# Batched matmul plus residual on one core: four batches for each transfer, four 4 MB rooms, loops of a whole ring

## What is computed

```python
x: (64, 128, 2048) fp32;  itok_B_0_15: (64,) int32 in 0..15;  L0_cond_weights: (16, 128, 128) fp32
W = weights[condition]
return x + jnp.einsum('bct,bcd->bdt', x, W)
```

## Time and profile before

| | |
|---|---|
| median of 3 runs | 322.93 us (322.84 to 416.34) |
| the profiled execution | 322.95 us, of which 321.2 us is the span |
| PE busy | 244.9 us (76% of the span), 512 matmuls |
| DVE busy | 146.7 us (46%), 64 sums |
| POOL busy | 19.0 us (6%) |
| DMA | 135.27 MB, 421 GB/s over the span |
| mean granted TensorE clock | 0.934 |

### The profile page before, as it was taken

One profiled execution on the slowest core, in us unless ns is written; L12 is line 12 of the kernel. 1 busy time (PEld: TensorE's weight loads), 2 busy tenths in 40 slices (PEclk: granted clock), 3 DMA queues, 4 the chain that ended last, 5 costly groups with the idle time before them and its releaser, 6 DMA issues.

```text
span 321.2 us, 2655 instructions
## 1 busy us (share of the span) xinstructions
PE 244.9 (76%) x512; PEld 102.1 (32%) x512; DVE 146.7 (46%) x64; POOL 19.0 (6%) x69
## 2 busy tenths in 40 slices
PE   0699999788868787696986867876869868678630
PEld 0244444233323233242332322332324323223310
DVE  0056757742545534346252555343552525553350
POOL 0000101000000000000000000000000000000000
PEclk9999999997989999789897999997997979999795
DMA  7999999999999999999999999999999999999994
GB/s 294 433 439 388 435 426 426 431 437 433 428 424 433 437 433 426 426 433 441 428 426 428 437 435 428 424 431 439 431 428 426 431 439 433 426 428 435 437 426 208
DMA packets 9362, 135.27 MB, mean 421 GB/s; under 512 B 1042, under 2 KB 1042, under 8 KB 1042
## 3 DMA queue, kind: packets, MB, share of 16 engines
q10 hardware_dynamic: 4754, 68.16, 49.8%
q1 hardware_dynamic: 4608, 67.11, 49.0%
HBM read 68.16 MB, written 67.11 MB: 421 GB/s over the span
## 4 chain that ended last, share of the span: by engine, by line
DMA 82%; PE 9%; DVE 3%; issue 1%; SPq 1%; DVEq 0%
DMA x_ring<-x 82%; PE product L97 9%; DVE x_ring L114 3%; SPq L70 1%; DVEq L114 0%; SPq L66 0%; DVEq L113 0%; SPq L65 0%; SPq L64 0%; SPq L69 0%
## 5 line engine op out<-in xcount | busy, mean ns | idle before, releaser
L97 PE MATMUL product<-x_ring,chosen_weights 128*128 x512 | 244.9, 637 | 63.3 <-DVE x_ring L114 43.4
L114 DVE TENSOR_TENSOR x_ring<-product,x_ring 128x2048 f32 x64 | 146.7, 2292 | 164.1 <-PE product L97 164.1
L97 PEld LDWEIGHTS product<-x_ring,chosen_weights 128*128 128x128 f32 x512 | 102.1, 203 | 205.3 <-issue 205.2
L83 POOL COPY chosen_weights<-weight_table 128x128 f32 x64 | 18.8, 293 | 269.0 <-DVEq L113 155.3
L138 POOL MEMSET const-float32-0.0<- 128x1 f32 x1 | 0.1, 98 | 0.1
L138 POOL MEMSET const-bfloat16-1.0<- 128x1 bf16 x1 | 0.1, 102 | 0.0
L138 POOL MEMSET const-uint8-127<- 128x1 uint8 x1 | 0.1, 102 | 0.0
L138 POOL MEMSET const-float32-1.0<- 128x1 f32 x1 | 0.1, 98 | 0.0
L138 POOL BASE_LOAD x1 | 0.0, 12 | 0.1
## 6 DMA issues: line engine op xcount, KB each, us to landing
x_ring<-x SPq DMA_DIRECT2D x32, 2048.0 KB, 19.4
out<-x_ring ACTq DMA_DIRECT2D x32, 2048.0 KB, 19.2
weight_table<-weights ACTq DMA_DIRECT2D x1, 1024.0 KB, 4.9
condition_row<-condition ACTq DMA_DIRECT2D x1, 0.2 KB
```

What stands on the lines that cost most here:

```text
L83: pool.tensor_copy(chosen_weights[b][:, :], weight_table[:, bass.ds(state * features, features)]).then_inc(weights_chosen, 1)
L97: last = pe.matmul(product[:, b % psum_slots, m * BANK_COLUMNS:(m + 1) * BANK_COLUMNS], chosen_weights[b][:, :], x_ring[:, bass.ds(ring_co ...
L114: dve.tensor_tensor(tile, product[:, b % psum_slots, :], tile, AluOpType.add).then_inc(psum_free, 1)
```

## The change

A group is now four batches: the host lays four side by side, a row is 32 KB, a group 4 MB, and there are 16 groups. `x_ring` has the same 16 MB, in four rooms. The loops of PE, DVE and POOL count four turns of 16 batches, so that one turn goes once round the ring and the addresses in `x_ring` don't depend on the turn. There are 16 `chosen_weights` instead of four, and each batch of a turn has its own `weights_chosen`, `product_done` and `sum_done` semaphore. DVE no longer raises a semaphore of its own for POOL; POOL waits for `product_done` itself. SP and ACT have no loop: their transfers are written out one by one. A load waits only for the store that last used its room. A store waits only for the last sum of its group. The last group is stored in four pieces, one for each batch, each as soon as its own sum is done.

```diff
-GROUP = 2
-IN_FLIGHT = 2
-RING_TURNS = 4
+GROUP = 4
+ROOMS = 4
-    per_turn = IN_FLIGHT * GROUP
+    per_turn = ROOMS * GROUP
-        x_ring = sbuf("x_ring", [channels, RING_TURNS * IN_FLIGHT * group_columns])
+        x_ring = sbuf("x_ring", [channels, ROOMS * group_columns])
...
+        def sums_wanted(turn, b):
+            return turn + (2 if b >= per_turn - psum_slots else 1)
         @block.sync
-            for g in range(IN_FLIGHT):
-                sp.sem_inc(x_loaded[g], 16)
-                sp.sem_inc(room_free[g], 16 * RING_TURNS)
-            with sp.Fori(0, turns) as turn:
-                for g in range(IN_FLIGHT):
-                    sp.wait_ge(x_loaded[g], 16 * (turn + 1))
-                    sp.wait_ge(room_free[g], 16 * (turn + 1))
-                    sp.dma_start(ring_group(turn, g), dram_group(x, turn, g)
-                                 ).then_inc(x_loaded[g], 16)
+            for g in range(groups):
+                room = g % ROOMS
+                if g >= ROOMS:
+                    sp.wait_ge(room_stored[room], 16 * (g // ROOMS))
+                sp.dma_start(x_ring[:, room * group_columns:(room + 1) * group_columns], x[g]
+                             ).then_inc(x_loaded[g % ROOMS], 16)
         @block.gpsimd
+            for b in range(per_turn):
+                pool.sem_inc(product_done[b], 1)
             pool.wait_ge(condition_loaded, 16)
             pool.wait_ge(table_loaded, 16)
-            pool.sem_inc(weights_free, per_turn)
...
-                    pool.wait_ge(weights_free, turn * per_turn + b + 1)
...
+                    pool.wait_ge(product_done[b], turn + 1)
...
         @block.tensor
+            for b in range(per_turn - psum_slots, per_turn):
+                pe.sem_inc(sum_done[b], 1)
...
+                    if b % GROUP == 0:
+                        pe.wait_ge(x_loaded[b // GROUP], 16 * (turn + 1))
+                    pe.wait_ge(weights_chosen[b], turn + 1)
+                    pe.wait_ge(sum_done[(b - psum_slots) % per_turn], turn + 1)
...
-                            x_ring[:, bass.ds(ring_column(turn, g) + within * time + m * BANK_COLUMNS,
-                                              BANK_COLUMNS)],
+                            x_ring[:, bass.ds(b * time + m * BANK_COLUMNS, BANK_COLUMNS)],
...
         @block.vector
+                    tile = x_ring[:, bass.ds(b * time, time)]
+                    dve.wait_ge(product_done[b], turn + 2)
-                    dve.sem_inc(weights_free, 1)
...
         @block.scalar
-            with act.Fori(0, turns) as turn:
-                for g in range(IN_FLIGHT):
-                    act.wait_ge(room_free[g], 16 * (turn + RING_TURNS))
-                    act.wait_ge(psum_free, turn * per_turn + (g + 1) * GROUP + psum_slots)
-                    act.dma_start(dram_group(out, turn, g), ring_group(turn, g)
-                                  ).then_inc(room_free[g], 16)
+            for g in range(groups - 1):
+                room, last = g % ROOMS, (g % ROOMS + 1) * GROUP - 1
+                act.wait_ge(sum_done[last], sums_wanted(g // ROOMS, last))
+                act.dma_start(out[g], x_ring[:, room * group_columns:(room + 1) * group_columns]
+                              ).then_inc(room_stored[room], 16)
+            g = groups - 1
+            for i in range(GROUP):
+                b = (g % ROOMS) * GROUP + i
+                column = (g % ROOMS) * group_columns + i * time
+                act.wait_ge(sum_done[b], sums_wanted(g // ROOMS, b))
+                act.dma_start(out[g, :, i * time:(i + 1) * time], x_ring[:, column:column + time]
+                              ).then_inc(room_stored[g % ROOMS], 16)
```

More of the change, by code:

```diff
@@ L39, in conditioned_residual @@
         table_loaded = sem("table_loaded")
[L42 to L57, removed]
+        x_loaded = [sem(f"x_loaded{g}") for g in range(ROOMS)]
+        room_stored = [sem(f"room_stored{r}") for r in range(ROOMS)]
+        weights_chosen = [sem(f"weights_chosen{b}") for b in range(per_turn)]
+        product_done = [sem(f"product_done{b}") for b in range(per_turn)]
+        sum_done = [sem(f"sum_done{b}") for b in range(per_turn)]
+        def sums_wanted(turn, b):
+            return turn + (2 if b >= per_turn - psum_slots else 1)
         block = ctx.enter_context(nc.Block())
@@ L122, in _ @@
                           ).then_inc(condition_loaded, 16)
-            with act.Fori(0, turns) as turn:
-                for g in range(IN_FLIGHT):
-                    act.wait_ge(room_free[g], 16 * (turn + RING_TURNS))
-                    act.wait_ge(psum_free, turn * per_turn + (g + 1) * GROUP + psum_slots)
-                    act.dma_start(dram_group(out, turn, g), ring_group(turn, g)
-                                  ).then_inc(room_free[g], 16)
-            for g in range(IN_FLIGHT):
-                act.wait_ge(room_free[g], 16 * (turns + RING_TURNS))
+            for g in range(groups - 1):
[10 more added lines that the diff above has]
+                              ).then_inc(room_stored[g % ROOMS], 16)
+            for r in range(ROOMS):
+                act.wait_ge(room_stored[r], 16 * (groups // ROOMS + (GROUP - 1 if r == g % ROOMS else 0)))
 def kernel(x, itok_B_0_15, L0_cond_weights):
```

10 lines of the change are left out of this document (3 added, 7 removed).

## The result

The changed kernel takes 320.21 us (median of 6 runs, 320.07 to 320.32); the kernel before took 322.77 in the same series. The ratio is 0.9921, 95% interval 0.9907 to 0.9934: 2.56 us less, clear of the noise, and under 2%. One of the six runs of the kernel before took 416.34 us, and the ratio leaves it out. The forecast was 322.3 us with a range of 319.5 to 327.0 and "within 2%" as the likeliest outcome. Its likeliest case by itself, 321 to 324 us, was missed at the fast end. The profiled execution took 320.21 us with a span of 318.4, so 1.8 us lie outside it, as before.

A forecast was written before the change was run, and what follows sets the result against it. DMA bytes over rate were taken to bound the kernel. Span 321.2 - 0.3 (start) + 0 + 0 = 320.9 us; with 1.75 outside, 322.65; less about 0.3 for longer rows, 322.3 us, range 319.5 to 327.0.

The forecast's parts named there:

- likeliest case: The sum's own case for the whole kernel: 321 to 324 us, 67 in 100.
- Longer rows carry: Faster rival: 1 us for packets, 0.7 at the start, the lagging engine's 3 us, giving 318.2; 14 in 100.
- The bound: Whole span: time is bytes over DMA rate, 135.27 MB at 431 GB/s, 313.9 us of 321.2.
- Bytes and packets: DMA rows twice as long, bytes unchanged: counted 0, range -1.0 to +0.5 us.
- Fewer transfers worth 0: The 64 big transfers become 35; their fixed costs are hidden behind queued transfers, so 29 fewer gain 0.
- Start, -0.3 us: SP's first load goes out near 0.8 us in place of 1.56: -0.3 us, between 0 and -0.7.
- up to 7 us of delay are covered: At the start, a later table landing costs nothing up to 7 us, as the first group lands near 15.4.
- Is there always something to move?: Queues with four rooms of 4 MB: loads stay 26.5 us of DMA work ahead, so engines never idle; 0.
- End: Last store in pieces keeps engines full, margin 5.7 us warm; one 4 MB lump would be 1.6 us too much; 0.
- The lagging engine: End of the run: one DMA engine, 3 us behind the others, still sets the end as before; 0.
- go cold for whole groups: Slower rival: PE at 1.2 GHz throughout the last group after long gaps, time 330.3 us; 6 in 100.
- Starvation: Slower rival: four coarse rooms leave both DMA queues dry at 12 handoffs of 1.3 us, giving 338; 4 in 100.

The follow-up runs named there:

- e1: Changed kernel with x and out laid out so that contiguous runs are 16 KB again, transfers still 4 MB: 321.10 us, ratio 0.9948.
- e2: Changed kernel with groups of 2 batches and 8 rooms of 2 MB, so 16 KB runs and 2 MB transfers: 321.68 us, ratio 0.9970.
- e6: Changed kernel with the table of matrices loaded first on SP's queue, ahead of x: 320.64 us, ratio 0.9940.
- e4: Changed kernel with the last group stored as one 4 MB transfer: 324.85 us, ratio 1.0078.
- e8: The 2-batch, 8-room variant e2 with 16 more semaphore raises on DVE for each batch, 1024 in all: 323.54 us, ratio 1.0027.
- the corners: Four kernels compared, old or new loops with groups of 2 or 4 batches; the new loops gave 1.0 us at 2 batches, 0.55 at 4.
- e7: Changed kernel with groups of 8 batches and two rooms of 8 MB, 64 KB runs: 372.70 us, ratio 1.1548.
- e12: Kernel before with groups of 4 batches, ring 2 turns deep, and the last group stored in four pieces: 320.95 us, ratio 0.9938.
- e11: The 2-batch, 8-room variant e2 with 1024 added semaphore raises on POOL: 331.10 us, ratio 1.0252.
- e5: Changed kernel with groups of one batch and 16 rooms of 1 MB, 8 KB runs: 324.51 us, ratio 1.0059.

## Why the prediction was right, and where it was not

**The number.** The time lies in the stated range, but by luck in part: the forecast took off 0.6 us, and 2.6 were gained. The likeliest case had 67 in 100 for 321 to 324 us, and 320.21 lies outside. What came is nearer to the rival "Longer rows carry", 14 in 100: of its three terms the packets gave 0.9 of 1 us, the lag 1.5 to 1.7 of 3, the start nothing of 0.7, and the lag fell mostly for a reason that this rival didn't have, the instructions.

**The bound.** Right: bytes over rate, engines at 9 tenths throughout. That is why so large a rewrite moved the time by 0.8%.

**Bytes and packets.** The size was taken as 0, with 0.3 us off at the end for what longer rows may give, and 1.0 as the far bound. Measured: 32 KB runs do move as one packet, and e1 puts their worth at 0.9 us, near that bound.

**Fewer transfers worth 0.** Nearly: e1 against e2 has 30 fewer and 480 fewer of the short packets, and gains 0.7 us (the intervals of the two just overlap). That is 0.02 us a transfer, a hundredth of the 2.0 us of the Trainium skill's rule (DMA: Bandwidth & Descriptors, "Anatomy of one DMA"), which by these runs can't be added up where another transfer always lies in line. The page made that rule for transfers issued by GpSimd, which the prediction doesn't say; here SP and ACT issue them.

**Start, -0.3 us.** Not seen. The first slice moved 313 GB/s against 294, but a slice counts packets by their starts, and 32 KB ones lift it; e2, with the same early first load and 16 KB packets, has 289. The table landed after 15.0 us and the indices after 16.2, and PE started at 18.99, where "up to 7 us of delay are covered" would have had it at 15.8. This step failed: x now shares the engines with the table from the first packet on, in packets four times as long. It cost nothing only because the stores' start had slack, as e6 shows.

**Is there always something to move?** Right. PE waits 39.5 us for loads in 12 waits, 3.3 a group where 5 were expected; PE's second turn began at 79.26, where the working has load 4 landing at 79; the last load landed at 292.23 and the last store at 317.9 (issued at 310.2, 7.7 to its landing), 25.7 us later, where the working had 26.5. The last sum ended at 310.2, expected near 312.

**End.** Right in kind, and the most telling term: with the last store whole, e4 loses 5.1 us, so that the cut of the last store is what made the whole change a gain. Its size was low: 1.6 us in the prediction's own terms, 2.4 with the measured lead, 3.4 in the profiled execution, where PE was 1.2 us slower than assumed, and 5.1 in the timed runs.

**The lagging engine.** This is the step that failed. The sum has "the lagging engine sets the end as before", a term of 0; the prediction gave its 3 us to a rival, which tied them to packets or transfers, and said "nothing ties it to their number". (At 316.8 the other 15 engines had started their last packets, not finished; they ended at 317.3.) The lag fell by 1.5 us by the completing packets, 1.7 by the slices, more than a half of the gain in the two traces. The changed kernel executes 1662 instructions, the one before 2655, and e8 shows that instructions that nobody waits for delay the last DMA engine, 1.3 ns each in its lag and 1.8 ns in the time. By that the 993 fewer would be worth 1.3 to 1.8 us; the corners give 0.55 to 1.0. In the table the lag at the end falls by 1.2 us for the new loops at 2 batches (961 fewer) and by 0.8 at 4 (740 fewer). The count of instructions is shown to be a cause, and not shown to be the measure: the growth is 0.75 to 1.5 ns for each executed instruction over the kernels of the table, and a register operation may weigh less than a semaphore raise, which was not tried alone.

**The rivals.** PE did not go cold for whole groups: it needed 15.6 to 16.8 us a group, against twice 7.13 at full clock, and the mean granted clock fell from 0.934 to 0.905, inside the slack. The working of that rival is a little high: 32 matmuls at 0.84 us in place of 0.45 are 12.5 us more, not 13.3; and what showed the slow stretch was their spacing, for the granted clock in that row reads 1.00. Starvation needs two rooms (e7).

**What stays open:** which part of an executed instruction sets a DMA engine back, and whether it would be there without the recording of a profile, since every run here has one. Nor is it known why it is one engine whose lag grows, or how much of the lag's fall with the old loops, 3.0 to 2.3 us from the kernel before to e12, is that of the packets and how much that of the 253 instructions.

## What to carry to other kernels

Where the DMA engines are full, count packets and transfers only after asking whether the queue is ever empty: they are then worth nanoseconds each (3.5 to 6 ns a packet here), and what counts is the end, where the last group in one store cost 5 us. Look at the last microseconds engine by engine: a tail of single packets is one engine behind the rest, and what burdens it can be work that no engine waits for. A loop made longer to save instructions can start to fetch its own code by DMA; look for an instruction queue with more than a few packets on the page.

## What the runs showed of the hardware

- 1024 semaphore raises in VectorE's idle time lengthened a DMA-bound kernel by 1.8 us (e8). They did it mainly through one of the 16 DMA engines, whose lag behind the others grows all through the run: 1.12 and 1.27 us per 100 us in kernels of 2655 and 2718 instructions, 0.39 to 0.69 in those of 1662 to 1718.
- Instruction fetches of 8 KB in a loop set one DMA engine back by some 0.6 us each, and 18 of them, most on one engine, lengthened the kernel by 9 us (e11); with the one fetch of 16 KB in the changed kernel came a jump of more than 1 us in one engine's lag.
- A contiguous run of 32 KB was moved as one packet. The rate in the middle changed from 431 to 432 GB/s.
- Two queues share an engine row by row: issued together with the loads, the 1 MB table of 8 KB rows landed after 7.7, 10.2, 15.0 and 24.5 us beside loads of 8, 16, 32 and 64 KB rows (e5, e2, the changed kernel, e7). The steps of 2.5, 4.8 and 9.5 us fit eight table rows an engine, each behind a load row that is 0.3, 0.6 and 1.2 us longer. With the first load issued 0.8 us later it landed after 4.8 beside 32 KB rows (e12).
